# A hand-scheduled transformer block: the opening loads in quarters, the rotation of the remote keys moved ahead, and the local rounds reordered

## The reference, cut to what matters

```
q_sem, k_sem = x @ Wq_sem, x @ Wk_sem            # 16 query heads, 4 key heads, 32 wide
q_geo, k_geo = rope(x @ Wq_geo), rope(x @ Wk_geo)
v = x @ Wv                                       # 4 heads, 64 wide
# the first 768 keys are averaged in 12 blocks of 64 (remote), the last 256 stay (local)
scores = (q_sem . k_sem2 + q_geo . k_geo2) / sqrt(32) * exp(logit_scale)[head]
out = softmax(masked scores) @ v2 @ Wo
x1 = layernorm(x + out)
x2 = layernorm(x1 + ffn(x1))                     # Hadamard transforms, gate, up, down
```

## Time and profile before

| | |
|---|---|
| median of 3 runs | 1581.56 us |
| the profiled execution's own time | 1581.24 us |
| its span in the trace | 1579.5 us |
| PE busy / DVE / ACT / POOL, share of the span | 97% / 66% / 39% / 30% |
| chain that ended last, by engine | PE 86%, DVE 9%, ACT 3%, issue 2% |
| granted TensorE clock, mean of the span | 0.999 of full speed |

### The profile page before, as it was taken

One profiled execution on the slowest core, in us unless ns is written; L12 is line 12 of the kernel. 1 busy time (PEld: TensorE's weight loads), 2 busy tenths in 40 slices (PEclk: granted clock), 3 DMA queues, 4 the chain that ended last, 5 costly groups with the idle time before them and its releaser, 6 DMA issues.

```text
span 1579.5 us, 26578 instructions
## 1 busy us (share of the span) xinstructions
PE 1533.4 (97%) x10280; PEld 1379.5 (87%) x10280; DVE 1037.2 (66%) x1771; ACT 616.3 (39%) x1257; POOL 470.2 (30%) x584
## 2 busy tenths in 40 slices
PE   6999999999998899999999999999999999999998
PEld 5987988887787688889999999999999999999997
DVE  7866776676676788875575475466466557557545
ACT  4253254236226644433333333343333333333332
POOL 5465456447338543500030030030040022003001
PEclk9999999999999999999999999999999999999999
DMA  7031122122222786587668677767766857766862
GB/s 272 8 122 52 34 89 93 34 81 100 70 68 94 266 320 253 214 300 274 239 217 289 229 248 249 272 211 250 276 234 229 308 206 245 285 233 224 277 229 95
DMA packets 92060, 307.44 MB, mean 195 GB/s; under 512 B 9888, under 2 KB 10272, under 8 KB 90144
## 3 DMA queue, kind: packets, MB, share of 16 engines
q1 hardware_dynamic: 90928, 301.54, 53.9%
q10 hardware_dynamic: 1008, 4.20, 0.7%
HBM read 255.37 MB, written 50.33 MB: 194 GB/s over the span
## 4 chain that ended last, share of the span: by engine, by line
PE 86%; DVE 9%; ACT 3%; issue 2%; DMA 0%; ACTq 0%; DVEq 0%; POOL 0%; POOLq 0%
PE ff_bank_b L1950 16%; PE ff_bank_a L1950 10%; PE ff_bank_c L1950 10%; PE ff_acc L106 7%; PE ff_acc L108 7%; PE ff_acc L107 7%; PE at_big L106 2%; PE at_big L108 2%; PE at_big L107 2%; PE at_mid L1093 2%; DVE ff_d_lo L1680 2%; PE at_acc L106 2%; PE at_acc L108 1%; PE at_acc L107 1%; ACT at_union L581 1%
## 5 line engine op out<-in xcount | busy, mean ns | idle before, releaser
L1950 PE MATMUL ff_bank_b<-ff_x_hi,ff_ring 128*128 128x256 f32 x1536 | 303.0, 280 | 7.6 <-DVE ff_c L1731 3.7
L1950 PEld LDWEIGHTS ff_bank_b<-ff_x_hi,ff_ring 128*128 128x128 f32 x1536 | 247.8, 188 | 9.9 <-issue 8.3
L1950 PE MATMUL ff_bank_b<-ff_x_lo,ff_ring 128*128 128x256 f32 x768 | 214.3, 279 | 0.0
L1950 PE MATMUL ff_bank_c<-ff_x_hi,ff_ring 128*128 128x256 f32 x1024 | 204.6, 283 | 0.6 <-DVE ff_ring L1670 0.6
L1950 PE MATMUL ff_bank_a<-ff_x_hi,ff_ring 128*128 128x256 f32 x1024 | 203.5, 282 | 1.1 <-DVE ff_ring L1670 0.8
L106 PE MATMUL ff_acc<-ff_d_hi,ff_h_hi 128*128 128x512 f32 x504 | 200.9, 399 | 1.8 <-DVE ff_d_lo L1680 1.8
L108 PE MATMUL ff_acc<-ff_d_hi,ff_h_lo 128*128 128x512 f32 x504 | 196.6, 390 | 0.0
L107 PE MATMUL ff_acc<-ff_d_lo,ff_h_hi 128*128 128x512 f32 x504 | 196.3, 389 | 0.0
L1950 PEld LDWEIGHTS ff_bank_a<-ff_x_hi,ff_ring 128*128 128x128 f32 x1024 | 165.3, 188 | 5.0 <-DVE ff_ring L1670 1.6
L1950 PEld LDWEIGHTS ff_bank_c<-ff_x_hi,ff_ring 128*128 128x128 f32 x1024 | 165.2, 188 | 2.9 <-issue 2.1
L1727 DVE TENSOR_TENSOR ff_c<-ff_bank_b,ff_c 128x512 f32<-128x512 f32 x64 | 44.2, 691 | 175.1 <-PE ff_bank_b L1950 174.9
(11 more groups left out here) (314 smaller groups left out, 3525.0 us busy)
## 6 DMA issues: line engine op xcount, KB each, us to landing
ff_ring<-gu_scratch SPq DMA_DIRECT2D x392, 512.0 KB, 5.0
gu_scratch<-ff_ring SPq DMA_DIRECT2D x56, 512.0 KB, 3.3
at_xt<-in_xt SPq DMA_DIRECT2D x4, 2048.0 KB, 8.3
at_xn<-in_x SPq DMA_DIRECT2D x32, 256.0 KB, 2.9
x_scratch<-at_x SPq DMA_DIRECT2D x32, 256.0 KB, 2.0
ff_raw<-in_wgu SPq DMA_DIRECT2D x8, 1024.0 KB, 5.7
at_wd_a<-in_wd SPq DMA_DIRECT2D x8, 512.0 KB, 4.3
mixed_scratch<-at_wd_a SPq DMA_DIRECT2D x8, 512.0 KB, 3.8
```

The lines of the kernel that those rows point to most:

```text
L1950: i = pe.matmul(bank[:, m, :], r[:, a, m, c, :], b[:, k, c, :], start=(k < 3 and m == 0 and c == 0 and b is x_hi and a == 0), stop=(m == 1 ...
```

## The change

Opening:

- xt and wkv are loaded in four quarters each, by inner chunk c; quarter c of both counts on one semaphore `first_in[c]`. SP counts `xt_in` itself, after it has waited for all four pairs, and issues the eight loads of wo only then. These count on one semaphore, and ACT waits for all eight before it rounds the first.
- PE makes the geometric keys with the chunk outside and the token tile inside (in all batches), in batch 0 waiting for each chunk. DVE sums the tokens of batch 0 chunk by chunk.
- rope, the small tables and the trigonometric tables have semaphores of their own.
- Quarters 0 and 1 of wq land in another tile (`y0`, held for the feed-forward block), so DVE can rotate the remote keys after `scale_wq(1)`, ahead of `scale_wq(2)` and both `lower_wq`.
- POOL scales quarter 3 of wq, before it makes lo of quarters 3 and 2; ACT rounds the quarters in the order 0, 1, 3, 2.

Local rounds, in every batch:

- POOL works out the inverse deviations of tiles 4 and 5 after pairs 3 and 4 (before: after pairs 1 and 3).
- ACT does `scale_x1` at the end of rounds 3, 4 and 7, behind `qo_hi` (before, in batches 0 to 2, in all three rounds ahead of it; in batch 3 in rounds 3 and 4).
- DVE takes in round 3 the maxima of the first pair before `transposed_queries(1)` and those of the second behind it (before: both behind it).

```diff
-        wq_raw = [union[:, 2 * D * c:2 * D * (c + 1)] for c in range(DC)]
+        wq_raw = [held["y0"][:, 2 * c:2 * c + 2, :].rearrange("p t e -> p (t e)") for c in (0, 1)] + [union[:, 2 * D * c:2 * D * (c + 1)] for c in (2, 3)]
...
+        SCALED = ((0, 512, DS), (512, 768, HALF), (768, 1024, HALF))
+        ROUNDED = (0, 1, 3, 2)
...
-            sp.dma_start(xt[:, :, :], io["xt"][0]).then_inc(xt_in.sem, 16)
-            for t, n in ((rope, "rope"), (small, "small"), (ident, "ident"), (cos_t, "cos_t"), (sin_t, "sin_t")):
+            for c in range(DC):
+                sp.dma_start(xt[:, c, :], io["xt"][0, :, c, :]).then_inc(first_in[c], 16)
+            sp.dma_start(rope[:], io["rope"]).then_inc(rope_in, 16)
+            for t, n in ((small, "small"), (ident, "ident")):
                 sp.dma_start(t[:], io[n]).then_inc(tab_in, 16)
+            for t, n in ((cos_t, "cos_t"), (sin_t, "sin_t")):
+                sp.dma_start(t[:], io[n]).then_inc(trig_in, 16)
+            for c in range(DC):
+                sp.wait_ge(first_in[c], 32)
+            sp.sem_inc(xt_in.sem, 16)
             for c in range(8):
-                sp.dma_start(wo_raw[c], io["wo"][:, c, :]).then_inc(wo_in[c], 16)
+                sp.dma_start(wo_raw[c], io["wo"][:, c, :]).then_inc(wo_in, 16)
...
-                        if tt == 0 and p in (1, 3):
-                            inverse_deviation(b, RT - 2 + p // 3)
+                        if tt == 0 and p in (3, 4):
+                            inverse_deviation(b, RT - 5 + p)
...
-            for c in range(2, DC):
-                pool.wait_ge(wq_hi_s, c + 1)
-                pool.tensor_tensor(wq_lo[:, c, :], wq_raw[c], wq_hi[:, c, :].bitcast(F32), ALU.subtract).then_inc(wq_lo_pool, 1)
+            pool.wait_ge(scale_done, 1)
+            pool.wait_ge(wq_in[3], 16)
+            for c0, c1, w in SCALED:
+                v = wq_raw[3][:, c0:c1].rearrange("p (h e) -> p h e", h=H)
+                pool.tensor_tensor(v, v, bc(scales[:, 0:H], 2, w), ALU.mult).then_inc(wq_scaled_pool, 1)
+            for n, c in enumerate(ROUNDED):
+                if c in (2, 3):
+                    pool.wait_ge(wq_hi_s, n + 1)
+                    pool.tensor_tensor(wq_lo[:, c, :], wq_raw[c], wq_hi[:, c, :].bitcast(F32), ALU.subtract).then_inc(wq_lo_pool, 1)
...
-            act.dma_start(wkv[:, :, :], io["wkv"]).then_inc(wkv_in, 16)
+            for c in range(DC):
+                act.dma_start(wkv[:, c, :], io["wkv"][:, c, :]).then_inc(first_in[c], 16)
...
-                    if i in (3, 4):
-                        scale_x1(b, RT - 5 + i)
-                    if more and i == 7:
-                        scale_x1(b, TILES - 2)
...
-                    if not more and i == 7:
+                    if i in (3, 4):
+                        scale_x1(b, RT - 5 + i)
+                    if i == 7:
                         scale_x1(b, TILES - 2)
...
-            for c in range(DC):
-                act.wait_ge(wq_scaled, 3 * c + 3)
+            for c in ROUNDED:
+                if c == 3:
+                    act.wait_ge(wq_scaled_pool, 3)
+                else:
+                    act.wait_ge(wq_scaled, 3 * c + 3)
                 act.activation(wq_hi[:, c, :], wq_raw[c], ACT.Copy).then_inc(wq_hi_s, 1)
...
             for c in range(8):
-                act.wait_ge(wo_in[c], 16)
+                act.wait_ge(wo_in, 16 * 8)
                 act.activation(wo_hi[:, c, :], wo_raw[c], ACT.Copy).then_inc(wo_hi_s, 1)
...
+                    for k in range(DC):
+                        dve.wait_ge(first_in[k], 32)
+                        for c, (c0, c1, n) in enumerate(((0, REMOTE, NB), (REMOTE, T, 1))):
+                            dve.tensor_reduce(xpool[:, k, NB * c:NB * c + n], xt[:, k, c0:c1].rearrange("p (n m) -> p n m", n=n),
+                                              AX.X, ALU.add).then_inc(xsum.sem, 1)
...
-                    if i == 3:
-                        transposed_queries(1)
...
-                        if i:
+                        if i == 3:
+                            local_maxima(i, (0,))
+                            transposed_queries(1)
+                            local_maxima(i, (1,))
+                        elif i:
                             local_maxima(i)
...
             pool_tokens(0)
             scale_wq(0)
             scale_wq(1)
+            dve.wait_ge(rope_in, 16)
+            rotate_pooled_keys(0)
+            scale_wq(2)
             lower_wq(0)
-            scale_wq(2)
             lower_wq(1)
-            scale_wq(3)
-            dve.wait_ge(wq_lo_s, 2)
             dve.wait_ge(zeroed, 1)
-            dve.wait_ge(tab_in, 16 * 5)
-            rotate_pooled_keys(0)
+            dve.wait_ge(tab_in, 32)
+            dve.wait_ge(trig_in, 32)
...
-                for t in range(RT):
-                    for c in range(DC):
+                for c in range(DC):
+                    if b == 0:
+                        pe.wait_ge(first_in[c], 32)
+                    for t in range(RT):
                         i = pe.matmul(qf[:, P * t:P * t + P], xt[:, c, P * t:P * t + P], wkv[:, c, 0:128],
-                                      start=(c == 0), stop=(c == DC - 1))
+                                      start=(c == 0 and t % 4 == 0), stop=(c == DC - 1), skip_group_check=True)
```

42 lines of the change are left out of this document (21 added, 21 removed).

## The result

The changed kernel is slower: 1591.56 us median of six runs (1589.05 to 1592.83) against 1582.29 us of the kernel before beside it (six runs, 1581.07 to 1584.05), ratio 1.0057 with a 95% interval of 1.0044 to 1.0069. The forecast was 1579.5 us, the range ended at 1583.0 us.

What follows compares the result with a forecast made beforehand. It saw PE's own chain and ACT-to-DVE meeting level at L1060, then waits in the rounds. From 1581.24 us, +2.1 - 2.7 - 1.4 = -2.0 us gave 1579.2 us, as median 1579.5 us; range 1576.2 to 1583.0 us.

Steps and rivals of the forecast that it cites:

- Quarters: Opening: the last wkv quarter lands at about 12.5 us and PE finishes the local keys at 21.3 instead of 26.4 us.
- ACT and POOL split the tokens some 3 us later; ACT has nothing else to do then and POOL would sit idle: Opening: the later token split, once all quarters are in, falls in idle time; no cost was counted.
- POOL's path, 30.4 us: Opening: POOL scales wq's last quarter and subtracts twice, ending at 30.4 us, when the first query projection starts.
- The output weights: Opening: ACT waits for the last wo slice, 28.3 us, so krot and PE's turn of the pooled keys move +2.1 us.
- rival D: Opening: a slow PE clock after the pause before 39 us adds 1.5 us, 1581.0 us in all; chance 0.12.
- The rounds: Local rounds of batches 0 to 2: shorter waits leave -0.9 us per batch, -2.7 us together.
- what is late next: Rounds: of 1.45 us gained at the output product, the chain through tp_lo and the exponentials leaves 0.9 us per batch.
- Rival A: Rounds: PE gives nothing back of the 1.45 us per batch, 1576.7 us in all; chance 0.17.
- E: Rounds: they give nothing, leaving only the opening's +2.1 us, 1583.7 us in all; chance 0.09.
- Batch 3: Round 4 of batch 3: qo_lo comes 1.45 us sooner and all behind it moves too, -1.4 us.
- Rival C: Keys in batches 1 to 3: matmuls changing their target each time run slower, 1596 us in all; chance 0.04.
- Rival B: Opening: wo's last slice lands by 26.3 us or ACT is not last at L1060, so no delay; 1577.5 us, chance 0.08.

Runs made afterwards that it cites:

- xt_own: Changed kernel with the token quarters counted apart from the key/value weights, which count on two semaphores, and all tables on one: 1587.01 us.
- after_kv_first: Changed kernel with ACT's copy of the local keys and rounding of the values of batch 0 ahead of the wo slices: 1587.85 us median, ratio 1.0031.
- kv_first: late_prep plus ACT's copy of the local keys and rounding of the values of batch 0 ahead of the wo slices: 1579.53 us own time.
- warm_only: late_prep plus 19 unneeded matmuls on zeros ahead of PE's first keys, ACT's order as before: 1579.66 us own time.
- rounds_only: Kernel before the change with only the new order of the local rounds: 1581.51 us median, ratio 0.9987.
- scale2_first: Changed kernel with DVE scaling quarter 2 of wq ahead of the rotation of the remote keys: 1588.56 us.
- warm_kv_first: kv_first plus 19 unneeded matmuls on zeros ahead of PE's first keys: 1577.98 us median, ratio 0.9971.
- late_prep: rounds_only with DVE's three feed-forward preparation instructions of batch 3 in round 9, not round 4: 1579.96 us median, ratio 0.998.
- warm12_kv_first: kv_first plus 12 unneeded matmuls on zeros ahead of PE's first keys: 1577.06 us median, ratio 0.9967.

## Why the prediction was wrong, step by step

- **Quarters, "PE gains 5.1 us, up to here": wrong.** The step held that "all bytes ahead of the last quarter of wkv are the same as now, so it lands at about 12.5 us". The bytes are the same, the packets are not; it landed at 14.86 us. PE did not even wait for it. The first quarter landed only at 11.09 us, the keys started at 11.22 us instead of at 7 to 9 us, and from there PE worked 14.0 us without a gap. The keys' end came at 25.2 us against 26.4 us, a gain of 1.2 us, not 5.1 us.
- **"ACT and POOL split the tokens some 3 us later; ACT has nothing else to do then and POOL would sit idle": this failed most.** It asked whether the two had time and not what they do to DVE. The prediction charged nothing for it. The split came 5.4 us later and lay on the six scales: 6.95 us instead of 2.62 us. `xt_own` shows it: without that overlap 2.9 us come back at the turn and 5.9 us at the products. The Trainium skill, SBUF — State Buffer, section on who interferes with whom, says that a DVE instruction with two inputs in SBUF and a GpSimd instruction that reads SBUF exclude each other for a whole instruction; the rows agree, and I had not weighed that rule. By it, moving POOL's work has a price on DVE even where POOL has time.
- **POOL's path, 30.4 us: wrong by 4.5 us.** (Its lower bound adds up to 30.1, not 29.9 us.) I followed quarter 3 alone. Its scaling took 2.63 us as forecast (2.7) and its subtraction 2.34 us (forecast 3.05), but it began at 22.53 us, 2.0 us late with its landing. The last link was quarter 2: POOL's wq_lo of it could not start before ACT rounded it at 30.39 us, behind DVE's rotation. The step left out that the rotation, moved ahead, now stands in front of a quarter that two engines wait for. The first projection came 4.6 us late. The order is the path of that delay and not its size: with the quarters alone it is as late (35.36 us), with the rotation behind quarter 2 too (35.32 us), and with the order but whole loads it is at 31.73 us. Most of the 4.6 us is DVE's late and stretched scaling.
- **The output weights, "the dearest term, +2.1 us": the wrong gate.** I let the last landing decide, 28.3 us; it was 29.49 us and decided nothing. ACT came to it at 33.80 us, for the same quarter 2. From there to krot it took 4.56 us, exactly as forecast, and krot to the turn 6.6 instead of 6.05 us. The turn moved by 8.1 us instead of 2.1. That everything behind ACT's chain moves with it was right (`after_kv_first`), as was "two chains meet at L1060" (`kv_first` and `warm_only`).
- **The clock, rival D: right mechanism, too small and too unlikely.** After the pause before the turned keys the clock fell; the price was 2.8 to 3.0 us, not 1.5, since PE ran most of the second projection at 1.2 GHz (its rows are slow up to 51.9 us, of 46.24 to 54.53 us). The 1.5 us were read from the first keys "though the granted clock reads 1.00 throughout"; the pace of these rows is that of the lower level for their first 3 us, so the 1.5 us were the price of one short slow stretch. The first slow start was hidden, as forecast: from the first projection to the turn of the local keys PE needs 7.4 us without its pause, 1.6 us more than before (30.34 to 36.10 us), but it then still waits 1.73 us at L1086. In `after_kv_first` and `xt_own`, where that wait is gone, nothing hides it.
- **The rounds: right.** Forecast -0.9 us a batch, measured -0.77, -0.74 and, with the stray wait in batch 2, -0.33; `rounds_only` has -0.7 in each. The step "what is late next" held in kind, by another wait than the one named: the gain of 1.45 us at the output product is cut by tp_lo, 0.52 us in round 3 and 0.26 us in round 5, more than by the exponentials, 0.28 us in round 6. Rival A (rounds keep all) and E (give nothing) fall with `rounds_only`.
- **Batch 3: -1.4 us forecast, -0.6 us measured.** qo_lo moved by 1.3 us, but "all behind it does" failed. The first of the three preparation instructions took 0.86 us instead of 0.16 us: it began at 503.81 us while POOL's division ran and ended at 504.67 us, with that division (504.65 us); in before it began behind it. The three took 2.35 us instead of 1.66 us. So tp_lo kept only 0.6 of the 1.3 us, PE came earlier than it, and the wait grew from 1.21 to 1.94 us. The rows of after:

```profile
503.20 0.68 DVE L916 TENSOR_TENSOR at_qo_lo<-at_tr,at_qo_hi 64x512 fp32r<-64x512 f32 x1 [0.30 <-ACT at_qo_hi L649]
503.81 0.86 DVE L1869 TENSOR_SCALAR h_ug_scale<-h_ug_scale 128x16 f32<-128x16 f32 x1
...
506.09 0.68 DVE L885 TENSOR_TENSOR at_tp_lo<-at_mid,at_tp_hi 128x512 fp32r<-128x512 f32 x1
506.91 0.47 PE L106 MATMUL at_tr<-at_tp_hi,at_v_hi 128*128 128x512 f32 x1 [1.94 <-DVE at_tp_lo L885]
```

- **Rival C** (key matmuls slower with the chunk outside) fell: batches 1 to 3 got shorter, none longer. **Rival B** (no hold) was right that the slices of wo don't hold ACT, and wrong in its cause and its sum: they landed later, not sooner, and ACT came later still.
- **The range** was too narrow on its upper side because every bound was set around one landing. No case priced POOL's work on DVE or let two engines wait for the same late quarter, and the slower side held 0.05 on a mechanism in the matmuls alone.

## What to carry to other kernels

When a step moves in one engine's order, list every consumer of what it is moved past: here the rotation went ahead of a quarter for which ACT and POOL both waited. Price an engine's extra work on its neighbour too: DVE and POOL working on SBUF at once stretch each other, and an idle POOL is not a free one. A load cut into parts may start its user sooner and still end later; look at what the queue beside it moves in the same time. A change that opens a pause in front of PE may pay for it twice, with the pause and with the clock behind it. Where two chains meet level, shorten both or neither. And follow single instructions from run to run: here own times differ by slow stretches that have nothing to do with the edit.

## What the runs showed of the hardware that I had not expected

- **DVE stands behind POOL's running instruction**: scales of 0.68 and 0.41 us became 2.00 and 2.57 us, an addition of 0.56 us 2.37 us; the other way round POOL's subtraction of 1024 columns took 3.31 us when it was issued at 31.52 us while DVE's wq_lo ran (to 32.62 us), and 2.34 us when POOL had begun first. It is not only for two inputs: DVE's scaling of the pooled sums (L719, one tensor input) took 1.05 us in before and ended with POOL's subtraction at 15.43 us; in after (L741), with POOL starting beside it, it took 0.19 us.
- **The quartered loads moved less at equal DMA share**: 317 against 399 GB/s from 8 to 12 us, with packets of a quarter of the size. That the size does it is not shown; over 30 us the two kernels are level.
- **The clock also falls without a wait.** In `kv_first` PE has no wait from 12.65 us up to the rounds of batch 0, and yet the clock falls at 47.2 us, towards the end of the 32 narrow products (48 columns) of 43.76 to 47.5 us:

```profile
44.00:47.00 3.00, 3.00 (x29) 3.00 (x29) 2.97 (x3) 0.00 (x0) 3.00 (x3) 1.00 0.00 0
47.00:50.00 3.00, 3.00 (x11) 2.18 (x11) 2.93 (x4) 0.81 (x1) 2.92 (x3) 0.53 0.00 0
```

The batch that holds such a stretch is 127.9 us long instead of 126.35. It stood in batch 0 of `kv_first`, `warm_only` and `scale2_first`, in batch 1 of `warm_kv_first` (173 to 177 us) and `xt_own` and in no batch of `late_prep`, `rounds_only` or before, with the same products in each. A like stretch stands at 534 to 538 us in `late_prep` and `rounds_only` and in neither before nor `warm12_kv_first`. Why it comes in one execution and not in another stays open. With the 6.9 to 8.3 us of the first keys it is a likely source of the 1 to 4 us by which runs of one kernel differ: the executions of before with a mean granted clock of 0.999 take 1581.1 to 1581.8 us, those with 0.996 take 1582.7 to 1585.1 us. The Trainium skill, TensorE: Matmul & The Clock Gate, section on the HAM clock gate, says that the same kernel can have a different number of slow matmuls from run to run; the rows of the keys agree.
